# The second dense layer of the attention's output as four jobs of one token tile, the first layer's jobs one step sooner

## What is computed

```python
x = x + tanh(g_xattn) * xattn(layernorm(x), ctx)      # 16 heads of 16; out @ W1 -> relu -> @ W2
x = x + tanh(g_ffn) * moe_ffn(layernorm(x))           # shared expert + 2 of 8 routed experts

# inside xattn, after softmax(q k / 4) v:
h = relu(out @ W1 + b1)      # 256 -> 512
return h @ W2 + b2           # 512 -> 256
```

## Time and profile before

| what | value |
|---|---|
| median of 3 runs | 1090.48 us (1089.4 to 1093.59) |
| the profiled execution's own time | 1090.56 us |
| its span, first to last instruction | 1088.8 us |
| busy: PE, PEld (weight loads), DVE, ACT | 96%, 48%, 60%, 53% of the span |
| mean granted TensorE clock | 0.995 of 2.4 GHz |

### The profile page before, as it was taken

How to read it: one execution, slowest core, us unless ns; L and a number is a source line. 1 busy time by engine, 2 the same in 40 slices (tenths; PEclk the granted TensorE clock), 3 DMA queues, 4 the chain that set the end, 5 groups by cost and what they waited for, 6 DMA issues and landing times. The chain is left out here.

```text
span 1088.8 us, 15032 instructions
## 1 busy us (share of the span) xinstructions
PE 1050.0 (96%) x5573; PEld 521.1 (48%) x5573; DVE 657.6 (60%) x907; ACT 574.5 (53%) x1065; POOL 201.1 (18%) x212
## 2 busy tenths in 40 slices
PE   5889999999999999999999999898999999999998
PEld 2443445444445433544434433224666666666665
DVE  3989786895687897678798588222642222222216
ACT  2138777886687777577777578762211111111111
POOL 4017400009000006300000040020011333333210
PEclk9989999999999999999999999999999999999999
DMA  6451220420211420302112100111920111111125
GB/s 170 107 156 24 42 62 1 121 61 1 61 33 29 122 48 13 62 1 60 37 26 61 41 20 2 59 58 50 368 89 25 49 39 49 49 45 44 39 71 181
DMA packets 38278, 70.11 MB, mean 64 GB/s; under 512 B 6848, under 2 KB 23360, under 8 KB 38208
## 3 DMA queue, kind: packets, MB, share of 16 engines
q1 hardware_dynamic: 30832, 56.42, 19.8%
q0 software_dynamic: 3744, 10.23, 3.0%
q10 hardware_dynamic: 3632, 2.51, 0.9%
HBM read 33.70 MB, written 9.31 MB: 40 GB/s over the span
## 5 line engine op out<-in xcount | busy, mean ns | idle before, releaser
L610 ACT ACTIVATE probs<-ring_ps 128x512 f32<-128x512 f32 (+1 forms) x832 | 443.1, 597 | 138.2 <-PE ring_ps L770 133.4
L883 DVE TENSOR_REDUCE mpart<-s_ps 128x2 f32<-128x1024 f32 x384 | 458.0, 1221 | 85.7 <-PE s_ps L757 85.7
L770 PE MATMUL ring_ps<-qst,kst 64*128 64x512 f32 (+1 forms) x832 | 233.3, 465 | 3.9 <-ACT probs L610 3.3
L785 PE MATMUL pv_ps<-probs,vp 128*32 128x512 f32 (+2 forms) x1664 | 222.3, 607 | 0.7 <-ACT probs L610 0.7
L770 PEld LDWEIGHTS ring_ps<-qst,kst 64*128 64x128 f32 (+1 forms) x832 | 100.8, 181 | 218.2 <-ACT probs L610 111.0
L757 PE MATMUL s_ps<-kst,qst 63*128 63x512 f32 (+1 forms) x1024 | 182.3, 400 | 8.3 <-DVE mpart L883 6.9
L1105 ACT ACTIVATE s_sb<-gu_ps 128x512 f32<-128x512 f32 x55 | 32.9, 597 | 256.7 <-PE gu_ps L1196 256.7
L1363 DVE TENSOR_TENSOR h_sb<-s_sb,gu_ps 128x512 f32<-128x512 f32 x55 | 37.8, 687 | 170.3 <-ACT s_sb L1105 170.2
L1196 PE MATMUL gu_ps<-wgu,xbT 128*128 x312 | 140.3, 592 | 0.0
L757 PEld LDWEIGHTS s_ps<-kst,qst 63*128 63x128 f32 x1024 | 92.2, 186 | 69.4 <-DVE mpart L883 43.7
L217 POOL TENSOR_SCALAR veps<-mv 128x4 f32<-128x4 f32 x8 | 1.9, 232 | 535.9 <-DVE mv L852 285.8
(11 more groups left out here) (183 smaller groups left out, 885.5 us busy)
## 6 DMA issues: line engine op xcount, KB each, us to landing
kst<-parts SPq DMA_DIRECT2D x45, 401.0 KB, 5.3
qst<-parts SPq DMA_DIRECT2D x48, 128.0 KB, 4.5
wgu<-in_WgT SPq DMA_DIRECT2D x16, 256.0 KB, 7.6
wgu<-in_WuT SPq DMA_DIRECT2D x16, 256.0 KB, 7.9
wd<-in_WdT SPq DMA_DIRECT2D x8, 512.0 KB, 9.7
wgu<-picked SPq DMA_DIRECT2D x8, 512.0 KB, 7.4
cold<-in_ctxT SPq DMA_DIRECT2D x3, 800.5 KB, 4.1
cold<-in_ctxT SPq DMA_DIRECT2D x6, 400.2 KB, 6.0
```

What stands on the lines that cost most here:

```text
L610: nc.scalar.activation(probs[0:w, m % NPB, h, :], ring_ps[0:w, bank(("st", idx)), :], ACT.Exp, scale=SCALE).then_inc(exp_done, 1)
L770: nc.tensor.matmul(ring_ps[0:w, bank(("st", idx)), :], kst[u % NKB][rows, h // 2, mt * P:mt * P + w], qst[u % NKB][rows, h // 2, :], start ...
L785: last = nc.tensor.matmul(pv_ps[32 * h:32 * h + c1 - c0, :], values[:, c0:c1], probs[0:w, m % NPB, h, :], start=(mt == 0), stop=(mt == MT ...
L883: nc.vector.tensor_reduce(mpart[:, :, p, t, q], s_ps[:, n % NSP], AX.X, ALU.max).then_inc(s_free, 1)
```

## The change

`W2` is cut into four jobs of one token tile each: 4 matmuls of 256 columns into the first half of a bank (1024 columns in all), and one DVE instruction on 128x256 per job. They stand at steps 11 and 12 of unit `hg == 0` and at steps 0 and 4 of unit `hg == 1`. The four `W1` jobs move from steps 7, 8, 9 and 11 to 6, 7, 8 and 9. For the last batch `last_jobs` has four `W2` jobs in place of two. The waits that named half 1 now name tile 3. `NT` is 4.

```diff
@@ schedule
-            for f, mt in enumerate((7, 8, 9, 11)):
+            for f, mt in enumerate((6, 7, 8, 9)):
                 at[mt].append(("W1", b - 1, f))
-            at[12].append(("W2", b - 1, 0))
+            for t, mt in enumerate((11, 12)):
+                at[mt].append(("W2", b - 1, t))
         if hg == 1 and b > 0:
-            at[0].append(("W2", b - 1, 1))
+            for t, mt in zip((2, 3), (0, 4)):
+                at[mt].append(("W2", b - 1, t))
...
-            [("W2", b, 0), ("W2", b, 1)])
+            [("W2", b, t) for t in range(NT)])
@@ ACT, take
-                        act.wait_ge(job_full, count(("W2", b - 1, 1)))
+                        act.wait_ge(job_full, count(("W2", b - 1, NT - 1)))
@@ TensorE, do
-                    _, b, half = job
+                    _, b, t = job
                     pe.wait_ge(free_act, freed["W1", b, F1 // P - 1])
-                    for i in range(2):
-                        t = 2 * half + i
-                        for k in range(F1 // P):
-                            last = nc.tensor.matmul(slot[:, i * D:(i + 1) * D], h1[:, k, t * P:(t + 1) * P],
-                                                    w2[:, k, :], start=(k == 0), stop=(k == F1 // P - 1))
+                    for k in range(F1 // P):
+                        last = nc.tensor.matmul(slot[:, 0:D], h1[:, k, t * P:(t + 1) * P], w2[:, k, :],
+                                                start=(k == 0), stop=(k == F1 // P - 1))
@@ VectorE, second_statistics
-                    dve.wait_ge(free_dve, freed["W2", b, 1])
+                    dve.wait_ge(free_dve, freed["W2", b, NT - 1])
@@ VectorE, do
-                    _, b, half = job
+                    _, b, t = job
                     dve.wait_ge(biased, NT * (b + 1))
-                    at = b * NT + 2 * half
-                    nc.vector.scalar_tensor_tensor(out=x1[:, at:at + 2, :].rearrange("p t d -> p (t d)"), in0=slot,
-                                                   scalar=tg[:, 0:1],
-                                                   in1=x1[:, at:at + 2, :].rearrange("p t d -> p (t d)"),
-                                                   op0=ALU.mult, op1=ALU.add).then_inc(free_dve, 1)
+                    at = b * NT + t
+                    nc.vector.scalar_tensor_tensor(out=x1[:, at, :], in0=slot[:, 0:D], scalar=tg[:, 0:1],
+                                                   in1=x1[:, at, :], op0=ALU.mult, op1=ALU.add).then_inc(free_dve, 1)
```

## The result

The changed kernel takes 1094.96 us (median of 10 runs, 1093.37 to 1096.66), the kernel before 1092.06 us beside it (10 runs, 1089.08 to 1095.94). The ratio is 1.0032, with a 95% interval of [1.0016, 1.0048]: slower by about 0.3%, where 0.07% faster was forecast. It lies inside the 0.5% that was named as no change, but outside the range of 1087.5 to 1092.8 us, and the difference has the other sign. The profiled execution took 1096.66 us against 1090.56, 6.1 us more.

What follows compares the result with a forecast made beforehand. TensorE, busy 96% of the span, was taken to set the length of job steps alone; -0.5 us in the loop and -0.27 at the first block's end gave 1089.8 us from 1090.56, range 1087.5 to 1092.8.

Steps and rivals of the forecast that it cites:

- Quarter step: Loop step holding a quarter `W2` job: 2.34 us plus 1.91 us for the job, 4.25 us in all.
- saved in the loop: Five changed steps per batch go from 21.42 to 21.25 us: 0.17 us a batch, 0.5 us for three.
- saved at the end of the block: After the last batch's final `W2`, VectorE's exposed read takes 0.484 instead of 0.751 us: 0.27 us saved.
- two plain steps lose their slack: In the loop, two plain steps lose 0.26 us of slack each; two added jobs pay a fixed 0.17 us each.
- the covers named for what costs nothing: VectorE's extra 0.43 us a batch, `W1` after ACT's copy of `OT`, and the row DMA all fit in existing time.
- Rival 1: Quarter steps in the loop take 4.08 us, saving 2.55 us, 2.8 with the end: 1087.7 us; chance 0.13.
- rival 2: VectorE's late bank read delays following steps: quarters 4.34 us, 1090.9 us, chance 0.15; above 1092.8 us, chance 0.04.
- the rule on VectorE tiles of 512 elements: Smaller VectorE reads of `W2` pay 0.217 us fixed each: 1.3 us lost if VectorE set the step; counted as nothing.
- signs that were named for a wrong prediction: Any of five steps off by over 0.1 us, first `W1` waiting for `OT`, or the second block changing length.
- The sum: Whole kernel: -0.5 - 0.27 = -0.8 us against 1090.56 us, giving 1089.8 us, 0.07% less.
- the five steps: Loop steps 6, 11 and 12 of `hg` 0, 0 and 4 of `hg` 1, each 4.25 us after the change.
- something not listed: Whole kernel: an unnamed effect that gives over 5.4 us back; chance 0.04.

Runs made afterwards that it cites:

- filling: Kernel before or changed kernel with TensorE matmuls nobody reads added where it idles or waits; medians from 1089.01 to 1094.40 us.
- first filling: Unread score matmuls in the 16 steps without a maximum search: 1094.40 us on the kernel before, 1093.73 us on the changed kernel.
- six with the second: Unread matmuls also in the last batch's waits: first pair 1094.07 us on the kernel before, 1092.09 us on the changed kernel.
- last_only_again: Kernel before with only the last batch's `W2` cut into four jobs, run a second time: 1093.33 us, ratio 1.0019.
- w1_only: Kernel before with only the `W1` jobs moved to steps 6 to 9, `W2` in two jobs as before: 1092.51 us, ratio 1.0019.
- last_only: Kernel before with only the last batch's `W2` cut into four jobs, the loop as before: 1095.27 us, ratio 1.0042.
- after_late1: Changed kernel with the first matmul of batch 0's first `W1` job done once more, about 0.8 us: 1091.57 us, ratio 1.0008.
- loop_only: Kernel before with quarter jobs and earlier `W1` in the loop only, last batch with two `W2` jobs: 1094.40 us, ratio 1.0021.
- again: The changed kernel, unaltered, measured and traced a second time: 1094.27 us, ratio 1.0024 to the kernel before.
- before_again: The kernel before, unaltered, as a control: 1091.86 us, ratio 1.0020.
- after_late2: Changed kernel with the first matmul of batch 0's first `W1` job done two times more, about 1.7 us: 1097.26 us.
- before_late7: Kernel before with the first matmul of batch 0's first `W1` job done seven times more, about 6.0 us: 1100.19 us, ratio 1.0081.

## Why the prediction was wrong

**Right: the account of the steps.** Quarter step 4.25 us, forecast 4.25; saved in the loop 0.48 us, forecast 0.5; saved at the end of the block 0.26 us, forecast 0.27. That two plain steps lose their slack while two jobs more pay a fixed part held, as did the covers named for what costs nothing: ACT's copy of `OT`, the row DMA and VectorE's longer work are on no path. Rival 1 (quarters at 4.08 us) and rival 2 (the bank late, 4.34 us) did not come; the rule on VectorE tiles of 512 elements, which the forecast took from the Trainium skill, VectorE: DVE Perf Modes, the section on the TRN2 errata, would have cost 1.3 us by the forecast's own working and cost nothing, for VectorE had idled before each of the sixteen reads. None of the signs that were named for a wrong prediction came: the steps fit, the first `W1` does not wait for `OT`, and the second block keeps its 332.0 us. The time was off all the same.

**Wrong: the term that was not in the sum.** The step that failed is "The sum. -0.5 - 0.27 = -0.8 us against the profiled execution's 1090.56 us". It took everything outside the five steps to stay as it was. The runs showed that TensorE's clock does not: it is granted at half rate in stretches at a few places of the program (near 40, 70, 695, 740 and 801 us), and which of them have one changes from execution to execution and from one program to the next. The pair near 695 and 740 us costs 2.45 + 2.34 = 4.8 us, and 16 of 20 runs of the changed kernel are at 0.989 or below against 16 of 137 of the kernel before. If each of these runs has that pair, it is 4.8 x (0.80 - 0.12) = 3.3 us, an estimate, against the 2.9 us between the medians and the 0.8 us that was gained. No chance had been given to this: "something not listed", at 0.04, was a gain of over 5.4 us, and every loss in the list was one of VectorE's read. The start from three runs added to the miss: the kernel before, 1090.48 us there, had a median of 1092.06 in ten. From that the forecast would be 1091.3 us, still 3.7 below what was measured.

The page had shown it. The mean clock was in the table, 0.995 and not 1.00, and the row PEclk had an 8 in its third slice; the windows read were of the loop alone, where it is 1.00. The spread of the three runs, 4.2 us, five times what the forecast was about, was written down as noise and not asked for its cause. It has one: among the runs of the kernel before, those at 0.997 took 1088.9 us in the mean and those at 0.989 1094.2 us.

**Shown and not shown.** It is shown that the loss of the first trace is time at the low clock, and that the loop of the change is 0.5 us shorter in every trace and the end of its block 0.26 us, where the two can be compared. That TensorE's idle time in the two places is needed for the low clock there is well supported: four of the eleven traces without filling have the stretch near 695 us and a fifth has it near 702, where its last unit stands, but none of the eight with filling; near 740 us eight of eleven have it, both with the first filling alone, and none of the six with the second; and none of 47 runs with both filled is at 0.989 or below, where last_only_again in the same set as 24 of them is in 6 of 12. The changed kernel itself was not run beside the filled ones.

It is not shown why the changed kernel meets the low clock so often. It is not the time since the first instruction: the last unit comes at 693.73 us in w1_only, with a low stretch behind it, and at 693.72 in last_only, without. But the same traces have one order that nobody tried by a run. Take the time from the start of the low stretch near 70 us to the last `pv` of the unit before the last. (The start is read from a window of 2 us: 70:72 at 0.73 has 2 x 0.27 / 0.5 = 1.08 us at the low clock, so it begins at 70.9.) For w1_only and then last_only:

```profile
70.00:72.00 2.00, 1.55 (x8) 0.77 (x6) 1.99 (x2) 1.45 (x3) 0.15 (x1) 0.73 1.08 202
693.73 1.06 PE L787 MATMUL pv_ps<-probs,vp 65*32 65x512 f32 x8
70.00:72.00 2.00, 1.55 (x9) 0.72 (x8) 1.92 (x2) 1.51 (x4) 0.09 (x1) 0.69 1.03 228
693.72 1.06 PE L787 MATMUL pv_ps<-probs,vp 65*32 65x512 f32 x8
```

| trace, none filled | low from, us | last `pv` of the unit, us | apart, us | low in the last unit |
|---|---|---|---|---|
| last_only_again | 72.9 | 694.28 | 621.4 | no |
| after_late1 | 71.2 | 692.61 | 621.4 | no |
| loop_only | 70.4 | 692.67 | 622.3 | yes |
| the changed kernel | 72.7 | 695.14 | 622.5 | yes |
| again | 70.2 | 692.75 | 622.6 | yes |
| w1_only | 70.9 | 693.73 | 622.8 | yes |
| last_only | 70.8 | 693.72 | 623.0 | no |
| the kernel before | 70.5 | 693.56 | 623.0 | no |
| before_again | 69.8 | 693.06 | 623.3 | no |
| after_late2 | 70.3 | 695.09 | 624.8 | no |
| before_late7 | 70.6 | 699.51 | 629.0 | yes |

The four between 622.3 and 622.8 us have the stretch, those on either side from 621.4 to 624.8 do not, before_late7 far off does, and the 0.5 us that the new loop saves lie between 623.0 and 622.5. So the gain itself may bring the last unit to where the clock falls. Eleven traces suggest this and do not prove it; by it last_only stands with the kernel before, and yet it is low in 11 of 19 runs. That stays open.

## What to carry to other kernels

Once the steps are tuned to a tenth of a microsecond, look at the granted clock of the whole span before a small change is forecast or judged, and compare runs at the same mean clock: here a gain of 0.8 us measured as a loss of 2.9. A stretch in which TensorE waits a little in every step is a place where the clock may fall, and here matmuls nobody reads kept the clock up, if they fitted into the wait: before a search 0.43 us of them did not make it longer than VectorE's own 1.22 us, 0.86 us did. Look at the whole row of the clock afterwards, for a low stretch can appear elsewhere, as it did near 770 us. Do that first, and then measure small edits on top.

## What the hardware showed that was not expected

- The clock fell with TensorE far from idle. Ahead of 697 us it was busy for 85% of 7 us, and no wait that the timeline names was longer than 0.54 us. The Trainium skill, TensorE: Matmul & The Clock Gate, section "HAM oscillation — how this bites in real kernels", speaks of avoiding long idle gaps of TensorE; the traces here show low stretches without one.
- The Trainium skill, TensorE: Matmul & The Clock Gate, section "What's actually happening", says that the gate judges how busy TensorE has been, and that this goes on freely and does not begin anew with the kernel. That agrees with the low stretch near 70 us: in the ten traces with none before it, it begins anywhere from 69.5 to 71.9 us, though the instructions up to there are the same. It also agrees with last_only having a low stretch near 740 us in one trace and none in the other.
- In the last unit a lower clock makes TensorE the bound of steps that ACT had set, which is why the stretch near 697 us costs 2.45 us: the step from the `pv` of 698.14 us took 4.54 us at the low clock, and its like in the kernel before, from 696.25, 3.08 us.
